# Attention on one Trainium2 core: ScalarE makes the high half of every fourth probability tile, GpSimd keeps the other three

## What is computed

```python
q = rmsnorm(...)   # 32 heads of 128
k, v = ...         # 8 key/value heads, each shared by 4 query heads, 512 context rows
scores = jnp.einsum('bhqd,bhkd->bhqk', q, k) * scale + attention_mask
attn = jax.nn.softmax(scores.astype(jnp.float32), axis=-1).astype(q.dtype)
out = jnp.einsum('bhqk,bhkd->bhqd', attn, v)
```

## Time and profile before

| | |
|---|---|
| median of 3 runs | 627.85 us (625.82 to 628.69) |
| the profiled execution | 627.91 us, span of its instructions 626.2 us |
| mean granted TensorE clock | 0.972 of full speed |
| busy: PE, DVE, ACT, POOL | 568.6, 407.3, 345.5, 348.2 us |
| attention tiles, first to last `masked_scores` | 319.89 to 501.67 us of the span |

### The profile page before, as it was taken

How to read it: one execution, slowest core, us unless ns; L and a number is a source line. 1 busy time by engine, 2 the same in 40 slices (tenths; PEclk the granted TensorE clock), 3 DMA queues, 4 the chain that set the end, 5 groups by cost and what they waited for, 6 DMA issues and landing times.

```text
span 626.2 us, 11602 instructions
## 1 busy us (share of the span) xinstructions
PE 568.6 (91%) x3232; PEld 277.2 (44%) x3232; DVE 407.3 (65%) x1038; ACT 345.5 (55%) x858; POOL 348.2 (56%) x370
## 2 busy tenths in 40 slices
PE   2999798599889849999976999999999999999997
PEld 0445344477654334444422444444444444444453
DVE  6895886365442774555569999999999920000783
ACT  4465847344333047676765777777777733243132
POOL 5990378579972606888864454544454543568011
PEclk9999999799988959999989999999999999999999
DMA  9995359999975504798979999999999995243001
GB/s 336 413 384 212 68 158 201 281 365 409 380 261 182 171 1 106 147 224 183 191 164 187 185 166 182 179 180 182 180 178 183 180 160 202 68 142 126 2 1 67
DMA packets 211622, 118.78 MB, mean 190 GB/s; under 512 B 188017, under 2 KB 196337, under 8 KB 208642
## 3 DMA queue, kind: packets, MB, share of 16 engines
q1 hardware_dynamic: 209122, 108.58, 68.3%
q0 software_dynamic: 2288, 9.70, 4.4%
q10 hardware_dynamic: 176, 0.04, 0.0%
HBM read 56.94 MB, written 15.20 MB: 115 GB/s over the span
## 4 chain that ended last, share of the span: by engine, by line
PE 53%; POOL 15%; DVE 13%; issue 11%; DMA 4%; ACT 3%; DVEq 0%; POOLq 0%; SPq 0%; ACTq 0%
PE ps L356 17%; PE ps L357 15%; PE ps L358 15%; POOL wsp L1305 6%; POOL hlr L1305 5%; PE ps L537 2%; POOL q_sb L1305 2%; DVE x_sb L1832 1%; PE ps L663 1%; DVE f32r L1726 1%; DVE stage L1864 1%; DMA stage<-in_first_chunks 1%; PE ps L830 1%; DMA r_dram<-f32r 1%; DMA stage<-in_moe,disp 1%
## 5 line engine op out<-in xcount | busy, mean ns | idle before, releaser
L1176 ACT ACTIVATE f32r<-f32r,mneg 128x512 f32<-128x512 f32 x128 | 91.5, 715 | 29.1 <-DVE mneg L1854 29.1
L1305 POOL TENSOR_TENSOR wsp<-stage,wsp 128x512 f16<-128x512 f32 x68 | 77.2, 1165 | 53.2 <-ACT wsp L1148 52.3
L1854 DVE CUSTOM_DVE_ANT_0 f32r<-ps,nmask 128x512 f32<-128x512 f32 x128 | 82.4, 680 | 1.6
L1437 POOL TENSOR_SCALAR hlr<-f32r,rinv 128x512 f16<-128x512 f32 x64 | 44.2, 699 | 48.3 <-DVE rinv L1859 45.1
L1437 POOL TENSOR_SCALAR stage<-f32r,rinv 128x512 f16<-128x512 f32 x64 | 43.6, 692 | 48.2 <-DVE rinv L1859 44.7
L1305 POOL TENSOR_TENSOR hlr<-f32r,hlr 128x512 f16<-128x512 f32 x36 | 41.2, 1156 | 44.2 <-ACT hlr L1257 33.3
L356 PE MATMUL ps<-q_sb 128*128 128x512 f16 x132 | 52.7, 399 | 12.7 <-POOL q_sb L1305 11.9
L356 PE MATMUL ps<-k_sb,q_sb 128*128 (+1 forms) x128 | 49.3, 385 | 11.6 <-DVE mneg L1854 8.9
L357 PE MATMUL ps<-q_sb 128*128 128x512 f16 x132 | 52.5, 398 | 0.0
L358 PE MATMUL ps<-q_sb 128*128 128x512 f16 x132 | 52.1, 395 | 0.0
L1864 DVE SCALAR_TENSOR_TENSOR stage<-f32r,rinv,stage 128x512 f16<-128x512 f32 x64 | 49.3, 807 | 2.5 <-POOL stage L1437 2.5
(11 more groups left out here) (359 smaller groups left out, 1431.8 us busy)
## 6 DMA issues: line engine op xcount, KB each, us to landing
stage<-in_wq SPq DMA_DIRECT2D x8, 1024.0 KB, 6.0
stage<-in_wo SPq DMA_DIRECT2D x8, 1024.0 KB, 4.9
q_sb<-in_moe SPq DMA_DIRECT2D x9, 768.0 KB, 8.4
xs_dram<-zeros SPq DMA_DIRECT2D x1, 5888.0 KB, 29.4
pT<-xs_dram SPq DMA_DIRECT2D x23, 256.0 KB
r_dram<-f32r SPq DMA_DIRECT2D x23, 256.0 KB
k_sb<-in_wkv SPq DMA_DIRECT2D x3, 1024.0 KB, 18.7
stage<-in_moe SPq DMA_DIRECT2D x4, 768.0 KB, 8.8
```

The source lines that it names most:

```text
L1176: act.activation(f32r[:, j % 4, :], f32r[:, j % 4, :], ACT.Exp, bias=mneg[:, j % 4:j % 4 + 1], scale=-1.0, accum_out=psum_col[:, j % 4:j % ...
L1305: return pool.tensor_tensor(dst_lo, src, dst_hi, ALU.subtract)
L1437: pool.tensor_scalar(halves(j)[:, 0, :], f32r[:, j % 4, :], rinv[:, 0, j % 4:j % 4 + 1], PSCALE, ALU.mult, ALU.mult).then_inc(s_ph, 1)
L1854: dve.tensor_tensor_reduce(f32r[:, j % 4, :], ps[j % 4][:, :], nmask[:, qt, :], 0.125, BIG, ALU.add, ALU.min, mneg[:, j % 4:j % 4 + 1]).th ...
```

## The change

ACT gets a function `prob_hi` of its own and makes the high half of tiles 3, 7, 11 and 15 of each round (`act_high`), with a semaphore of its own, `s_pha`. POOL's loop skips these tiles, and its count `s_ph` now grows by 12 a round. DVE's `prob_lo` waits for `s_pha` in these tiles and for `s_ph` in the others. On ACT the new work stands behind `scaled_inverses` and ahead of the first exponential of the next group, that is at the head of every even turn. It takes the scaled inverse that ACT has just written, so it waits for ACT's own `s_sc`, and for `s_pT` of its slot.

```diff
+            def prob_hi(j, freed):
+                if freed is not None:
+                    act.wait_ge(s_pT[j % 8], freed)
+                act.activation(halves(j)[:, 0, :], f32r[:, j % 4, :], ACT.Copy, scale=rinv[:, 1, j % 4:j % 4 + 1])\
+                   .then_inc(s_pha, 1)
+
+            def act_high(g, j, first):
+
+                act.wait_ge(s_sc, 8 * g + j // 2 + 1)
+                if first and j < 8:
+                    act.wait_ge(s_qT[3], 16 * KVH)
+                    act.wait_ge(s_wql, 4 * (KVH + 1))
+                    prob_hi(j, None)
+                else:
+                    prob_hi(j, 32 * g + 16 * (j // 8))
 
             def attention(g, first):
                 for j in range(4 * REP):
...
                     if j % 2 == 0 and (not first or j >= 2):
                         scaled_inverses((j - 2) % 4, 8 * g + j // 2 - 1)
+                    if j % REP == 0 and (not first or j > 0):
+                        act_high(g, j - 1, first)
                     exponentials(j, k)
...
             scaled_inverses(2, 8 * KVH - 1)
+            act_high(KVH - 1, 4 * REP - 1, False)
             o_hi(4 * KVH - 4, 0)
...
-            for j in range(8):
+            by_pool = [j for j in range(8) if j % 4 != 3]
+            for j in by_pool:
                 prob_hi(j, 0, True)
             with pool.Fori(1, 2 * KVH) as v:
-                for j in range(8):
+                for j in by_pool:
                     prob_hi(j, v, False)
...
-                dve.wait_ge(s_ph, k + 1)
+                if at % 4 == 3:
+                    dve.wait_ge(s_pha, 4 * g + at // 4 + 1)
+                else:
+                    dve.wait_ge(s_ph, 12 * g + at // 4 * 3 + at % 4 + 1)
```

More of the change, by code:

```diff
@@ L306, in xattn_ffn_kernel @@
         s_hx = sem("s_hx")
-        s_hg = sem("s_hg")
+        s_pha = sem("s_pha")
         s_hh = sem("s_hh")
@@ L1859, in inverse_sums, with prob_lo @@
                 dve.reciprocal(rinv[:, 0, j:j + 2], psum_col[:, j:j + 2]).then_inc(s_r0, 1)
-            def prob_lo(j, k, pair):
+            def prob_lo(j, g, at, pair):
                 dve.wait_ge(s_sc, pair + 1)
-                dve.wait_ge(s_ph, k + 1)
+                if at % 4 == 3:
+                    dve.wait_ge(s_pha, 4 * g + at // 4 + 1)
+                else:
+                    dve.wait_ge(s_ph, 12 * g + at // 4 * 3 + at % 4 + 1)
                 dve.scalar_tensor_tensor(out=halves(j)[:, 1, :], in0=f32r[:, j % 4, :], scalar=rinv[:, 1, j % 4:j % 4 + 1],
@@ L1871, in attention @@
                         for j in range(2):
-                            prob_lo((a - 4 + j) % 16, 16 * g + a - 4 + j, pair - 2)
+                            prob_lo((a - 4 + j) % 16, g, a - 4 + j, pair - 2)
                     if not first or p >= 1:
@@ L1880, in _ @@
                 attention(g, False)
-            end = 16 * KVH
             for j in range(2):
-                prob_lo(12 + j, end - 4 + j, 8 * KVH - 2)
+                prob_lo(12 + j, KVH - 1, 12 + j, 8 * KVH - 2)
             inverse_sums(2, 8 * KVH - 1)
             for j in range(2):
-                prob_lo(14 + j, end - 2 + j, 8 * KVH - 1)
+                prob_lo(14 + j, KVH - 1, 14 + j, 8 * KVH - 1)
             dve.wait_ge(s_lw, 2)
```

## The result

The changed kernel takes 632.48 us (median of 4 runs, 632.07 to 634.1) against 627.72 us of the kernel before (median of 4 runs). The ratio is 1.0085 with a 95% interval of 1.0055 to 1.0114: slower by 0.85%, or 5.3 us on 627.72 (3.5 to 7.2). The profiled execution took 634.1 us, its span 632.3.

The account below looks back on a forecast made before the run. The prediction took ACT's chain to bound even turns, DVE odd turns, and SP's transposes pairs 40 to 63. The terms summed to 28 d - 2.7 us, +5.1 at d = 0.28, giving 633.0 us, range 629.3 to 636.2.

Parts of the forecast that it names:

- What binds the even turn: Attention stage: ACT's chain through both exponentials and the sum holds the reciprocal, giving 2.97 us; DVE binds the odd turn.
- the stall: DVE's first `prob_lo` stands still while POOL works; dropping POOL's second tile gives back 0.17 us per even turn.
- d: Delay of the even turn's first exponential behind ACT's new copy: 0.28 us, bounds 0.11 to 0.37, paid 28 times.
- Round 0: Turns there are bound by DVE; three even turns save some 0.15 us each without POOL's second tile: -0.45 us.
- SP: SP's transposes, 5.82 us a group, held pairs 40 to 63; at the changed pace of 5.90 they no longer would.
- The forecast gaps of SP: In the changed profile SP should show small gaps between transposes, and POOL no wait for landings.
- Behind the stage: After the last tile `o_hi` stands behind the new copy, so PE's `residual` waits 0.3 us.
- The cheap copy: ACT's copy runs like `o_hi` and starts at once, d below 0.21: 628.3 to 631.0 us; chance 0.17.
- The port and the transposes: DVE's late `prob_lo` holds the reciprocal; even turn falls to 2.65, SP sets the end: 627.4 us; chance 0.11.
- ACT blocked by a landing: ACT's copy waits for its slot's transpose, exponentials behind it: 635 to 638 us; chance 0.12, shared with a dearer copy.

Follow-up runs that it names:

- GpSimd's part alone: Kernel before, with GpSimd leaving out every fourth high half from tile 8 on and ACT getting no copy; ratio 1.0005 to the kernel before.
- a quicker SP: Changed kernel with SP's loop over the transposes written out with constant waits; ratio 1.0123 to the kernel before, stage 185.54 us.
- the two flat kernels: SP's transpose loop written out with constant waits, on the kernel before (ratio 0.9997, stage 177.93 us) and on the changed kernel (1.0123, 185.54 us).
- SP flat: SP's transpose loop written out with constant waits; with the changed kernel's copy moved to the odd turn, 625.01 us, 0.9978 of the kernel before.
- two kernels here: Changed kernel with `o_hi` behind the even turn's second exponential: ratio 1.0070 to the kernel before; the same with SP's loop written out: 0.9933.
- the waits turned: Changed kernel with only the copy's waits reordered, `s_pT` first and `s_sc` last; ratio 1.0115 to the kernel before, stage 186.37 us.
- the kernel with everything moved: Changed kernel with SP's loop written out, `o_hi` behind the second exponential and the copy waiting for `s_pT` before `s_sc`; 619.78 us, 0.9887 of the kernel before.
- the kernel of the early starts: Changed kernel with SP's loop written out and `o_hi` behind the second exponential, copy's waits left with `s_sc` first; 622.17 us, 0.9933 of the kernel before.

## Why the prediction was right

Predicted were 633.0 us, +5.1; measured 632.48, and +5.3 by the ratio.

- **What binds the even turn.** The 0.03 us between the sum and the reciprocal and the 0.23 us behind it were read as a wait on ACT. GpSimd's part alone shows it: the low halves got 0.17 us shorter and the turn did not. One reading beside it was off: the odd turn's low half was no case of the stall, though it too ended 0.54 us behind GpSimd. It took 0.76 us, as a low half does without GpSimd's second tile.
- **d.** The terms were a start at 0.39, a duration of 0.70, and d = 0.28. Measured: a start at 0.35 or 0.43 by halves, 0.722 us in each of 32 copies, and d = 0.27 or 0.35. In the mean it was (162.91 - 154.63) / 28 = 0.296, from 343.27 and 506.18. That 0.39 came out as the mean start was in part luck: one step of 0.08 us was taken, and there were two, 0.03 and 0.12. The duration is nearer to the exponential (0.72) than was taken; the estimate of 706 ns by the Trainium skill, page "ScalarE: Activation LUTs", section "What ACT_TABLE_LOAD costs", was 16 ns low.
- **Round 0.** -0.45 predicted, -0.55 measured (23.30 to 22.75).
- **SP.** The pace of 5.91 is slower than SP's 5.82, no landing was waited for, and a quicker SP changes nothing (185.54 and 185.66). The forecast gaps of SP did not come: it issued back to back and worked off its lag. For the kernel before a quicker SP would save 2.5 us of the stage, by the trace. Without this term the sum would have been too high by that much; between the two flat kernels the change costs 7.6 us of stage.
- **Behind the stage.** 0.3 us were predicted. `residual` moved from 3.96 us to 4.25 us (506.18 to 510.43) after the last pair's start.
- **The rivals.** The cheap copy did not come (0.722 us). The port and the transposes decide only in kernels where ACT's chain is shortened. ACT blocked by a landing had its mechanism right and its case wrong: not in the changed kernel, but in those with quicker turns. Its threshold was added up wrongly: two groups of 5.62 and 0.34, less 2.79, are 8.8, and less the landing 5.5, not 5.9. In the two kernels where ACT waited for landings with SP's loop as it was, the lag stood near 5.5 from tile 64 to tile 112.

## What to carry to other kernels

An engine with idle time is not free to take work: look where in its order the idle time lies and who waits for the instruction behind it. Here ACT had 0.39 us ahead of an exponential, the copy needed 0.62 and its start, and the rest came out on every group; two tiles further on, in the turn without `o_hi`, the same work cost less than a tenth of that (with SP flat, 0.6 us of stage in place of 7.6).

Where a faster part runs into a slower queue, a change is paid against the queue's pace and not against the part's: 7.6 us of stage became 5.2, and moving `o_hi` in the changed kernel took 5.1 us off its stage (185.66 to 180.61), but 12.2 with a quicker SP (185.54 to 173.34).

An instruction that waits for a buffer should not stand ahead of work that others wait for, on an engine that is on the path: in two kernels here it made PE pause for 2.0 and 2.2 us, and in one of them the clock fell behind the pause.

## What the runs showed of the hardware

- A register instruction between two waits shows between dependent instructions. From the end of the scaled inverse to the copy it was 0.03 us in the groups where nothing had to be computed, and 0.12 in the others:

```profile
420.29 0.20 ACT L1181 ACTIVATE rinv<-rinv 128x2 f32<-128x2 f32 x1
420.52 0.72 ACT L1186 ACTIVATE hlr<-f32r,rinv 128x512 f16<-128x512 f32 x1
```

  The groups with 0.12 are the first and the last of a round, where the trace has a register instruction between the two waits of the copy. With the waits turned nothing stands between, and yet it was 0.09 in all groups of rounds 1 to 7, so the order of the waits counts as well; why isn't shown.
- A wait that ends just behind the instruction ahead of it costs more than its own length: in the kernel with everything moved the reciprocal starts 2.57 us into the even turn and 2.56 into the odd one, and yet the even turn is 0.17 longer (397.04 to 399.85, 399.85 to 402.49), as it is in the kernel of the early starts. All fourteen traces agree on a floor: no first `masked_scores` of a pair in rounds 1 to 7 starts less than 0.26 us behind the end of ACT's sum. Where the reciprocal starts 0.03 behind the sum, `masked_scores` follows it by 0.23 or 0.24; where 0.15, by 0.12; where 0.22 or more, by 0.07 or 0.08. That the three waits behind the reciprocal are worked through only when its own has ended would explain it; it wasn't tried apart.
- PE's granted clock fell from 1.00 to 0.50 of full speed behind a pause of 2.2 us, and stayed there until 504 us, eight matmuls in all, some 1.7 us more than at full speed; behind a pause of 2.0 us in another kernel it did not fall.
- Four DMA transposes of 256 KB each take SP 5.82 us to issue with register waits in a loop and 5.52 with constants, and they land 3.3 us after their issue in both kernels. That constant time to land speaks for the queue's issue, and not for its data, as the limit of the kernel before; it wasn't tried apart.
